# A fused attention block: q's row transfers issued together, KT_0 moved a slot earlier, and the first steps reordered

## The reference, cut to what matters

```python
def _L0_ffn_ref(x, w_freq_real, w_freq_imag, bias):
    w = jax.lax.complex(w_freq_real, w_freq_imag)
    x_freq = jnp.fft.fft(x, axis=-1)
    y_freq = jnp.einsum('bnd,do->bno', x_freq, w)
    y = jnp.real(jnp.fft.ifft(y_freq, axis=-1))
    return y + bias
def _L0_attn_ref(x, Wq, Wk, Wv, Wo, bo):      # 16 heads of 8, on the left 128 features
    ...
    energy = jnp.einsum('nqhd,nkhd->nqkh', q, k)
    att = jax.nn.softmax(energy / scale, axis=2)
    out = jnp.einsum('nqkh,nkhd->nqhd', att, v)
    return out.reshape(N, S, E // 2) @ Wo.T + bo
x = x + 0.5 * _L0_ffn_ref(_layernorm(x), ...)
x = x + _L0_attn_ref(_layernorm(x), ...)
x = x + 0.5 * _L0_ffn_ref(_layernorm(x), ...)
```

## Time and profile before

| | |
|---|---|
| Median of 3 runs | 315.94 us (314.96 to 318.23) |
| The profiled execution | 318.33 us, of it 316.4 us span |
| PE busy | 298.1 us, 94% of the span |
| ACT busy | 259.3 us, 82% |
| DVE busy | 189.4 us, 60% |
| POOL busy | 97.6 us, 31% |
| Granted PE clock | full speed in all 40 slices |
| DMA | 49.86 MB, mean 158 GB/s |

### The profile page before, as it was taken

The page is one execution under the profiler, slowest core; times in us unless marked ns, Lnnn a source line. Parts: engine busy times, 40 slices in busy tenths (PEclk is TensorE's granted clock), DMA queues, the critical chain, the costliest instruction groups (busy, mean ns, idle before and its releaser), DMA issues.

```text
span 316.4 us, 8826 instructions
## 1 busy us (share of the span) xinstructions
PE 298.1 (94%) x3445; PEld 113.7 (36%) x3449; DVE 189.4 (60%) x550; ACT 259.3 (82%) x287; POOL 97.6 (31%) x112
## 2 busy tenths in 40 slices
PE   8888899899999999999998999899998999998996
PEld 5644333233333333333333333233332333232333
DVE  0687525767774778467774778368764653460255
ACT  2214989999999889898997989798998999999921
POOL 6644611043604152313604251403600340034005
PEclk9999999999999999999999999999999999999999
DMA  7835663146357373835465363626462474112102
GB/s 195 323 135 185 216 249 152 38 166 228 125 194 256 109 228 111 286 139 202 134 207 197 137 200 116 187 78 222 135 198 75 164 237 166 38 45 90 36 33 68
DMA packets 26563, 49.86 MB, mean 158 GB/s; under 512 B 2064, under 2 KB 14736, under 8 KB 24720
## 3 DMA queue, kind: packets, MB, share of 16 engines
q1 hardware_dynamic: 25824, 48.78, 44.9%
q10 hardware_dynamic: 688, 0.40, 0.7%
HBM read 31.34 MB, written 17.83 MB: 155 GB/s over the span
## 4 chain that ended last, share of the span: by engine, by line
PE 63%; DMA 14%; DVE 10%; issue 6%; ACT 5%; POOL 1%; SPq 1%; PEldq 0%; ACTq 0%; DVEq 0%
PE misc L716 23%; PE ot L824 22%; PE scores L796 11%; DMA QS<-q_scr 10%; ACT probs L666 5%; DMA left_scr<-left_blocks 3%; PE scores L683 2%; DVE left_blocks L964 2%; PE scores L716 2%; PE scores L690 1%; DVE lh L955 1%; DVE kp L983 1%; DVE kp L981 1%; DVE VS L1028 1%; POOL rstd L545 1%
## 5 line engine op out<-in xcount | busy, mean ns | idle before, releaser
L666 ACT ACTIVATE probs<-scores 128x1024 f32<-128x1024 f32 x256 | 243.8, 1029 | 24.1 <-PE scores L796 21.1
L824 PE MATMUL ot<-probs,VS 128*32 128x512 f32 x1024 | 134.0, 594 | 3.9 <-ACT probs L666 2.9
L796 PE MATMUL scores<-QS,KS 32*128 32x512 f32 x512 | 64.8, 495 | 4.5 <-DMA QS<-q_scr 3.7
L796 PEld LDWEIGHTS scores<-QS,KS 32*128 32x128 f32 x512 | 24.5, 181 | 111.7 <-ACT probs L666 100.2
L1015 DVE SCALAR_TENSOR_TENSOR x_out<-misc,rstd,x_out 128x256 f32<-128x256 f32 x28 | 13.6, 484 | 47.2 <-PE misc L716 43.8
L824 PEld LDWEIGHTS ot<-probs,VS 128*32 128x32 f32 x1024 | 30.7, 109 | 27.6 <-ACT probs L666 7.0
L558 POOL TENSOR_TENSOR x_out<-x,half_bias 128x512 f32<-128x512 f32 x7 | 9.0, 1287 | 90.7 <-DVE x L1010 90.7
L543 POOL TENSOR_SCALAR veps<-mv 128x4 f32<-128x4 f32 (+1 forms) x25 | 5.7, 228 | 95.9 <-DVE mv L944 95.9
L716 PE MATMUL misc<-half_ffn,xT 128*32 128x256 f32 x448 | 33.1, 387 | 0.0
L716 PE MATMUL misc<-half_ffn,xT_in 128*32 128x256 f32 x400 | 27.9, 385 | 1.8 <-DVE half_ffn L1186 1.3
L545 POOL TENSOR_TENSOR rstd<-veps,power 128x4 f32<-128x4 f32 (+1 forms) x25 | 25.2, 1008 | 2.1
(11 more groups left out here) (126 smaller groups left out, 259.9 us busy)
## 6 DMA issues: line engine op xcount, KB each, us to landing
KS<-k_scr SPq DMA_DIRECT2D x14, 512.0 KB, 4.2
QS<-q_scr SPq DMA_DIRECT2D x14, 512.0 KB, 4.5
x_in<-x SPq DMA_DIRECT2D x8, 512.0 KB, 6.5
xT_in<-x_t SPq DMA_DIRECT2D x8, 512.0 KB, 7.3
k_scr<-kp SPq DMA_DIRECT2D x8, 512.0 KB, 2.8
q_scr<-qp SPq DMA_DIRECT2D x8, 512.0 KB, 3.7
x_scr<-x_blocks SPq DMA_DIRECT2D x7, 512.0 KB, 3.5
xT<-x_scr SPq DMA_DIRECT2D x7, 512.0 KB, 4.5
```

The source lines that it names most:

```text
L666: nc.scalar.activation(probs[u % PRING][:, :, :], scores[u % SRING][:, :, :], ACT.Exp, scale=SCORE_SCALE).then_inc(exp_done, 1)
L796: last = mm(scores[(u + j // 2) % SRING][:, j % 2, :], KS[b % 2][rows, slot, kt * P:(kt + 1) * P].bitcast(F32R), QS[b % 2][rows, slot, :]. ...
L824: last = mm(ot[COL * j:COL * (j + 1), :], VS[b % 2][:, kt, h, :], probs[(u + j // 2) % PRING][:, j % 2, :], start=s % 8 == 0, stop=s % 8 == 7)
```

## The change

It has four parts.

1. The tables. In `STEADY`, KT_0 moves from slot 0 to slot 15 of the batch before (two batches ahead); slot 0 then holds KT_1 and F1_0a, slot 1 only F1_0. Batch 1 keeps the old slots 0 and 1 (`FIRST`). `LATE` keeps KT_1 alone in slot 0. `BEGIN` is rewritten: the halves of k and q no longer stand in pairs, and QT_1 comes in slot 8.
2. SP's list. Both transfers of q's rows are issued together, ahead of the load of leftT. The store of the second half of an output comes ahead of the next loads of x. In the first batch k's rows come ahead of q's store.
3. The prologue. The statistics of batch 0 come in one piece behind the second fold. F1 of batch 1 is evacuated in one piece, and its statistics come behind the guard's maxima. ACT makes `half_bias` after its last copies for the folds; POOL's first addition of it comes behind the first `rstd`.
4. ACT squares q of batch 1 ahead of slot 10 instead of slot 7.

```diff
-STEADY = {0: [("KT_0", 1, RIGHT), ("F1_0a", 2, LEFT)], 1: [("F1_0", 2, LEFT), ("KT_1", 1, RIGHT)],
+STEADY = {0: [("KT_1", 1, RIGHT), ("F1_0a", 2, LEFT)], 1: [("F1_0", 2, LEFT)],
...
-          14: [("F2_3a", -1, LEFT)], 15: [("F2_3", -1, LEFT)]}
+          14: [("F2_3a", -1, LEFT)], 15: [("F2_3", -1, LEFT), ("KT_0", 2, RIGHT)]}
...
-BEGIN = {1: [("LT", 1, LEFT)], 2: [("KT_0", 1, LEFT), ("KT_1", 1, RIGHT)], 3: [("QT_0", 1, LEFT), ("QT_1", 1, RIGHT)],
+BEGIN = {1: [("LT", 1, LEFT)], 2: [("KT_0", 1, RIGHT), ("F1_0a", 2, LEFT)], 3: [("F1_0", 2, LEFT)],
+         4: [("KT_1", 1, RIGHT), ("F1_1a", 2, LEFT)], 5: [("F1_1", 2, LEFT)], 6: [("QT_0", 1, RIGHT), ("F1_2a", 2, LEFT)],
...
-LATE = {0: [("KT_0", 1, RIGHT)], 1: [("KT_1", 1, RIGHT)],
+LATE = {0: [("KT_1", 1, RIGHT)],
...
             for it in range(1, B):
+                if it >= 2:
+                    store_out(it - 2, 1)
                 if it + 3 < B:
                     load_x(it + 3)
-                if it >= 2:
-                    store_out(it - 2, 1)
...
                 if it + 1 < B:
-                    q_in(it + 1, slice(0, 1))
+                    q_in(it + 1)
                 if it + 2 < B:
                     leftT_in(it + 2)
-                if it + 1 < B:
-                    q_in(it + 1, slice(1, None))
                 store_out(it - 1, 0)
...
+            rstd_of(0, 1)
             pool.wait_ge(bias_set, 1)
             pool.wait_ge(x_loaded[0], 16)
-            add_row(x1[0], x_in[0], half_bias, early_biased, slice(0, 2))
-            rstd_of(0, 1)
+            add_row(x1[0], x_in[0], half_bias, early_biased, slice(0, 1))
+            add_row(x1[0], x_in[0], half_bias, early_biased, slice(1, 2))
...
-                    if s == (2 * (8 if it == B - 2 else 10) if it else 2 * 7):
+                    if s == (2 * (8 if it == B - 2 else 10) if it else 2 * 10):
                         square(qp, sq_q, qp_step, it + 1)
...
-            norm0_stats(0, range(0, 2))
...
-            norm0_stats(0, range(2, T))
+            norm0_stats(0)
...
+            run_jobs(PROLOGUE, T)
+            for t in range(T):
+                evacuate(f"F1_{t}", 1)
+            run_jobs(PROLOGUE, 2 * T + 1)
+            run_jobs(PROLOGUE, 2 * T + 2)
             dve.wait_ge(row_ready, 1)
             nc.vector.tensor_copy(KS[0][:, 0, :].bitcast(F32R), row_banks[0]).then_inc(first_k_set, 1)
-            run_jobs(PROLOGUE, T + 6)
-            run_jobs(PROLOGUE, T + 7)
+            run_jobs(PROLOGUE, 2 * T + 3)
+            dve.wait_ge(evacuated, evac_count(f"F1_{T - 1}", 1))
+            for t in range(T):
+                norm_stats(1, x1[1], t, t == T - 1)
+            norm_moments(1, 2)
             guard(0)
```

More of the change, by code:

```diff
@@ L74 @@
           12: [("F2_1a", -1, LEFT), ("F2_1", -1, LEFT)], 13: [("F2_2a", -1, LEFT), ("F2_2", -1, LEFT)],
-          14: [("F2_3a", -1, LEFT)], 15: [("F2_3", -1, LEFT)]}
-BEGIN = {1: [("LT", 1, LEFT)], 2: [("KT_0", 1, LEFT), ("KT_1", 1, RIGHT)], 3: [("QT_0", 1, LEFT), ("QT_1", 1, RIGHT)],
-         4: [("F1_0a", 2, LEFT), ("F1_0", 2, LEFT)], 5: [("F1_1a", 2, LEFT)], 6: [("F1_1", 2, LEFT), ("F1_2a", 2, RIGHT)],
-         7: [("F1_2", 2, RIGHT)], 8: [("F1_3a", 2, LEFT), ("F1_3", 2, LEFT)], 9: [("V_0", 1, RIGHT)],
-         10: [("V_1", 1, LEFT), ("N", 1, RIGHT)]}
-LATE = {0: [("KT_0", 1, RIGHT)], 1: [("KT_1", 1, RIGHT)],
+          14: [("F2_3a", -1, LEFT)], 15: [("F2_3", -1, LEFT), ("KT_0", 2, RIGHT)]}
+FIRST = {**STEADY, 0: [("KT_0", 1, RIGHT), ("F1_0a", 2, LEFT)], 1: [("F1_0", 2, LEFT), ("KT_1", 1, RIGHT)]}
+BEGIN = {1: [("LT", 1, LEFT)], 2: [("KT_0", 1, RIGHT), ("F1_0a", 2, LEFT)], 3: [("F1_0", 2, LEFT)],
+         4: [("KT_1", 1, RIGHT), ("F1_1a", 2, LEFT)], 5: [("F1_1", 2, LEFT)], 6: [("QT_0", 1, RIGHT), ("F1_2a", 2, LEFT)],
+         7: [("F1_2", 2, LEFT), ("F1_3a", 2, RIGHT)], 8: [("F1_3", 2, RIGHT), ("QT_1", 1, LEFT)],
+         10: [("N", 1, RIGHT), ("V_0", 1, LEFT)], 11: [("V_1", 1, LEFT)]}
+LATE = {0: [("KT_1", 1, RIGHT)],
         2: [("WO_0", -1, LEFT), ("WO_1", -1, RIGHT)], 3: [("WO_2", -1, LEFT), ("WO_3", -1, RIGHT)],
@@ L100, in slots_of @@
         ahead = [(f"F1_{t}", 2) for t in range(T)]
-        jobs = [(f"F1_{t}", 1) for t in range(T)] + [("LT", 1)] + ahead[0:3] + [("KT", 1), ("QT", 1)] + ahead[3:4] + [("N", 1)]
+        jobs = [(f"F1_{t}", 1) for t in range(T)] + [("LT", 1)] + ahead + [("KT", 1), ("QT", 1), ("N", 1)]
         return {s: [(name, d, LEFT)] for s, (name, d) in enumerate(jobs)}
@@ L106, in slots_of @@
         return dict(enumerate(jobs + [[(f"F2_{t}", -1, LEFT)] for t in range(T)]))
-    table = {0: BEGIN, B - 2: LATE, B - 1: END}.get(it, STEADY)
+    table = {0: BEGIN, 1: FIRST, B - 2: LATE, B - 1: END}.get(it, STEADY)
     return {s: [(name, d, half) for name, d, half in jobs if it + d < B] for s, jobs in table.items()}
@@ L494, in _ @@
             k_out(1)
+            k_in(1)
             q_out(1)
-            k_in(1)
             q_in(1)
@@ L625, in _ @@
                 nc.scalar.copy(copy[:, :, :], half_bank(bank)).then_inc(ffn_copied, 1)
-            act.wait_ge(bias_loaded, 16)
-            nc.scalar.mul(half_bias[:, :], bias_raw[:, :], 0.5).then_inc(bias_set, 1)
             for piece, bank, copy in ((5, scores[0][:, 0], even[2]), (6, scores[0][:, 1], odd)):
@@ L630, in _ @@
                 nc.scalar.mul(copy[:, :, :], half_bank(bank), 0.5 / E).then_inc(ffn_copied, 1)
+            act.wait_ge(bias_loaded, 16)
+            nc.scalar.mul(half_bias[:, :], bias_raw[:, :], 0.5).then_inc(bias_set, 1)
             act.wait_ge(pick_loaded, 16)
@@ L1003, in evacuate @@
                     if b == 0 and i < 2:
-                        dve.wait_ge(early_biased, 1)
+                        dve.wait_ge(early_biased, i + 1)
                     else:
@@ L1204, in _ @@
             norm_moments(0, 2)
-            for s in range(T, T + 6):
-                run_jobs(PROLOGUE, s)
+            run_jobs(PROLOGUE, T)
[3 more added lines that the diff above has]
+            run_jobs(PROLOGUE, 2 * T + 2)
             dve.wait_ge(row_ready, 1)
             nc.vector.tensor_copy(KS[0][:, 0, :].bitcast(F32R), row_banks[0]).then_inc(first_k_set, 1)
-            run_jobs(PROLOGUE, T + 6)
-            run_jobs(PROLOGUE, T + 7)
+            run_jobs(PROLOGUE, 2 * T + 3)
[3 more added lines that the diff above has]
+            norm_moments(1, 2)
             guard(0)
```

## The result

Timed side by side, the changed kernel has a median of 314.61 us (313.87 to 315.57, 13 runs), the kernel before 316.88 (314.96 to 321.52, 13 runs). The ratio is 0.9942, with a 95% interval of 0.9919 to 0.9965: 0.6% faster. The prediction, 313.2 against 315.94, was a ratio of 0.9913. The direction is right, but a third of the forecast gain did not come. The ratio leaves out the three longest executions of the kernel before (320.50 to 321.52) as slow; by the plain medians the gain is 2.27 us. The profiled execution took 314.27 us.

A forecast was written before the change was run, and what follows sets the result against it. PE was taken as the bound, busy 94% of the span, with time won where it stands still or is held to ACT's pace. Terms -2.9 + 0 + 0.2 + 0.3 - 0.3 = -2.7 gave 313.2 us from 315.94, range 310.8 to 316.2.

The forecast's parts named there:

- part 1: Batch ends: issuing both transfers of q's rows together, ahead of leftT's load, was to win 2.9 us (-3.7 as lower bound).
- The wait for leftT: KT_0 in slot 15, at batch ends: leftT, loaded behind both q transfers, would hold it, 0.31 + 0.48 = +0.79 us.
- The forecast's sign: At the five batch ends: leftT lands 6 to 8 us after issue, PE idle under 0.5 us before KT_0.
- the -3.70: PE's idleness ahead of the next batch's score products at the batch ends, 3.70 us in all, taken as gone.
- the step shrinks: The profiled execution's 2.4 us above the median; shrinks to nearly nothing if shorter runs have shorter batch-end waits.
- Part 2: One job less in slot 1, one more in slot 15: 0 at batch ends (-1.0 to +1.0), +0.2 us in batch 6.
- Part 3: Batch 0's table: +0.3 us, two stalls gone (-1.0) against a new wait of about 1.3; bounds -1.0 to +1.3.
- ACT's wait: Batch 0, slot 5: ACT's square of k waits for KT_1's rounded part, delaying the exponentials; costs about 1.3 us.
- Part 4: The prologue: guard's maxima one us earlier, partly lost to POOL's later addition and later statistics; -0.3 us, bounds -0.6 to +0.25.
- leftT as the wait: Rival at all five batch ends: leftT lands late and KT_0 in slot 15 stops PE; slower, 319.2 us; chance 0.08.
- rows that land no earlier: Rival at batch ends: a slow transfer tail sets q's landing, the 3.7 returns; about +0.2, 316.1 us; chance 0.15.
- All waits go: Rival: no leftT wait, batch 0 wins 1.0, prologue wins 0.6; about -5.3, 310.6 us; chance 0.30.

The follow-up runs named there:

- the second execution of before: The kernel before with no edit, profiled a second time: median 316.77 us, ratio 0.9981 (0.995 to 1.0012).

## Why the prediction was right and wrong

By the ratio the forecast was 2.74 us, and 1.84 came (0.0058 of 316.88; by the interval 1.1 to 2.6; by the plain medians 2.27). The terms, each measured by itself, add up: part 1 -2.8 to -3.3, batch 0 about +1.05 (33.62 to 33.76 against 32.50 to 32.73), batch 6 +0.46, prologue -0.46. Together that is -1.75 to -2.25.

*Part 1* came out near the size predicted, but by luck: two errors met. The wait for q's rows went, as forecast. The wait for leftT, +0.79, did not come: KT_0 never waits for it, and in the seven profiles with part 1 and KT_0 in slot 15 leftT lands at least 0.5 us before PE reaches KT_0. The +0.79 rested on the step "the same bytes land by the same time with the two swapped". The transfers' landing, from issue, in the changed kernel, first q's rows (all transfers), then leftT:

```profile
DMA to landing us min/median/max: 3.6/4.4/5.7
...
DMA to landing us min/median/max: 3.3/5.4/6.2
```

leftT behind both of q's transfers landed within 6.2, where the earlier trace rows have up to 6.5 behind one; in the other profiles with part 1 it took up to 7.0. The forecast's sign, 6 to 8 us, was too late: here it took 4.7 to 6.2 at the batch ends. At the end of batch 1 it landed at 97.1 (91.59 + 5.5), where q's last rows landed at 98.35 before (92.35 + 6.00). In the other direction, the -3.70 was one execution's. The sentence that the step shrinks if shorter executions have shorter waits was right, but "to nearly nothing" was not: the second execution of before still lost 2.5 in batches 1 to 5 against the changed kernel (174.69 - 172.15 = 2.54). The rule of the Trainium skill that was weighed there (DMA: Bandwidth & Descriptors, section "Queues, rings and completion order") says that one ring's descriptors are consumed in order, but also that a later one may finish its write before an earlier one. So "leftT cannot pass q's rows" is more than it states. In this case leftT did not pass them: at the end of batch 1 its 97.1 is later than q's rows (96.2 at most: 89.88 + 1.18, and 5.1 for the slower of the pair), and at all batch ends of the eleven profiles with part 1 it landed behind them. The +0.79 was in no run.

*Part 2* was right for batches 1 to 5 (172.14 against 172.13). In batch 6, +0.2 was +0.46, the end of its bounds: KT_1 still starts 0.16 later behind KT_0, and the emptied slot gives back 0.23 of the 0.45.

*Part 3 is the step that failed*, +0.3 against +1.05. The size lies within its bounds, whose +1.3 allowed for stalls that return elsewhere, but no stall was named. ACT's wait was right to 0.1: 1.26 on PE, the products 3.62 apart for 3.6 forecast. What failed is "spread out, each job finds its predecessor evacuated". V_1 in slot 11 waits for V_0's evacuation, which stands in DVE's program behind the guard's maxima: N and V_0 share slot 10, N first, so DVE works off the guard's seven small operations, the first at 54.57 and the last at 56.06, before it copies V_0 at 56.13, and V_1 starts at 56.65. That is the 0.86. The job order that the table gives to PE is also the order of DVE's evacuations, and I had followed it for k and q only. The runs bear out both: the square moved, 1.24 back; V_0 and V_1 a slot earlier and ahead of N, 0.70 back. With the stalls that went (0.8 to 1.05) they make up the +1.05.

*Part 4* was -0.3 and measured -0.46 to the first exponential, from two terms that were both undersized. POOL's late addition, with the statistics in one piece and the later `half_bias`, costs about 0.55, not 0.25. Without it the guard's first maximum starts 1.27 earlier behind `half_ffn` than before (14.75 instead of 16.02), where 1.0 was taken; with it, 0.73 earlier. Of either, 0.27 is lost between the maxima and the first exponential, for which I have no cause, so 1.0 and 0.46 are left. LT of batch 1 started at 33.43 instead of 34.81, not near 34.2. Of these 1.38, 0.77 are the earlier `half_ffn` of that execution, and the other 0.61 is what the forecast allowed. But the left half, which was to hold LT, did not: it ended at 33.15 (32.05 + 1.10), and LT has no idle row.

Of the rivals, leftT as the wait fell at every batch end, and so did rows that land no earlier. *All waits go* was right that no wait takes the place of q's, and wrong for the square of k. Its version of batch 0 exists: it is the run with the square later and the values ahead of the guard.

## What to carry to other kernels

A table that spreads jobs out on one engine also orders the evacuations on the next: for each job moved, look at what stands ahead of its predecessor's evacuation there, above all a chain of small operations such as a guard. A wait for a transfer that is read from one profile has a spread of its own; a second profile of the same kernel tells more of its size than a price worked out from one. And a fixed place in another engine's list (here ACT's square of k) must move with the job that feeds it: one number was worth 1.2 us.

## What was not expected of the hardware

At the batch ends q's second transfer, of 512 KB, lands later when leftT's load, of 256 KB, has been issued ahead of it in the same queue than when it goes ahead of leftT: 5.5 to 7.3 us from its issue in the second profile of before and 5.3 to 6.7 in the changed kernel with part 1 taken out, against 4.8 to 5.7 for the slower of the pair in the changed kernel and at most 6.4 in the eleven profiles with part 1. leftT itself is slower by less behind both: at the batch ends 4.2 to 7.0 in those eleven profiles (median 5.2), against 3.5 to 6.5 in the three profiles that have it behind one (median 4.4). At the end of batch 4 the second profile of before shows (KB each, us to landing):

```profile
QS<-q_scr SPq DMA_DIRECT2D x1, 512.0 KB, 7.3
leftT<-left_scr SPq DMA_DIRECT2D x1, 256.0 KB, 3.6
```

Why leftT takes so much from the transfer behind it was not tried. The executions of before span 314.96 to 321.52 us, those of the changed kernel 313.87 to 315.57, and with part 1 taken out they span 315.48 to 321.04 again: with the wait the spread goes too. And the start of `half_ffn` lies between 11.21 and 12.29 in seven profiles with the prologue of the changed kernel, and between 11.47 and 12.46 in six with the old one, which no edit explains; the 0.77 in the table above is within that spread.
